# Products of a zero tile in TensorE's waits, k_lo ahead of prod, and VectorE's set-up moved, in a hand-scheduled attention kernel

## What is computed

```python
# stage 0: attention of side (queries) over x (keys, values), plus each query's own key and value
q = (side + b_self) @ Wq + bq
k = concat([x + b_prev, side + b_self]) @ Wk + bk ;  v = concat([x, side]) @ Wv + bv
score_prev = q . k[:256] * SCALE, masked by key position >= seq_len ;  score_self = (q * k[256:]).sum * SCALE
x = x + (softmax([score_prev, score_self]) @ v) @ Wo + bo
# stage 1: pooled mixing of the rows of x
scores = tanh(x @ W1 + b1) @ v ;  mask by the batch's kind (prefix, postfix, all but itself)
x = x + softmax(masked scores) @ x / count
```

## Time and profile before

| quantity | value |
|---|---|
| median of three runs | 279.0 us |
| time of the profiled execution | 281.62 us |
| span of its profile, first to last instruction | 279.9 us |
| TensorE busy with matmuls | 238.4 us, 85% |
| VectorE busy | 184.4 us, 66% |
| ScalarE busy | 156.6 us, 56% |
| GpSimd busy | 76.3 us, 27% |
| mean granted TensorE clock | 0.95 of full speed |

### The profile page before, as it was taken

The page is one execution under the profiler, slowest core; times in us unless marked ns, Lnnn a source line. Parts: engine busy times, 40 slices in busy tenths (PEclk is TensorE's granted clock), DMA queues, the critical chain, the costliest instruction groups (busy, mean ns, idle before and its releaser), DMA issues.

```text
span 279.9 us, 6089 instructions
## 1 busy us (share of the span) xinstructions
PE 238.4 (85%) x2100; PEld 187.4 (67%) x2100; DVE 184.4 (66%) x384; ACT 156.6 (56%) x297; POOL 76.3 (27%) x87
## 2 busy tenths in 40 slices
PE   2986898599979999999999989999999769886732
PEld 2984787367758777877788768777787455563622
DVE  2659655457469758875887588758985885335631
ACT  4351223376477557755785667557856546772430
POOL 8026011013025103610451035103511330316111
PEclk9999669599999999999999999999999997999977
DMA  5469636913865096609560946096409410011011
GB/s 152 103 235 233 138 112 182 210 31 115 242 142 188 5 248 134 228 16 252 119 227 20 256 108 225 18 246 118 150 33 261 95 72 2 8 34 37 0 40 37
DMA packets 28021, 35.50 MB, mean 127 GB/s; under 512 B 4440, under 2 KB 24416, under 8 KB 28000
## 3 DMA queue, kind: packets, MB, share of 16 engines
q1 hardware_dynamic: 27360, 33.12, 44.6%
q0 software_dynamic: 640, 2.10, 2.0%
HBM read 20.26 MB, written 14.69 MB: 125 GB/s over the span
## 4 chain that ended last, share of the span: by engine, by line
PE 59%; DVE 13%; DMA 9%; issue 8%; ACT 5%; SPq 3%; POOL 1%; ACTq 0%; DVEq 0%; POOLq 0%
PE ps_any L1080 20%; PE ps_any L1134 10%; PE ps_max L1108 9%; PE ps_any L1087 6%; DMA k_rows<-k_spill 5%; PE ps_exp L1121 4%; DVE s_max L887 4%; DMA k_spill<-k_lo 3%; PE ps_any L1184 3%; PE ps_any L1240 2%; DVE bv_cast L854 2%; SPq L418 1%; ACT pt L623 1%; PE ps_any L1200 1%; PE ps_any L1166 1%
## 5 line engine op out<-in xcount | busy, mean ns | idle before, releaser
L887 DVE TENSOR_REDUCE s_max<-ps_max 128x4 f32<-128x1024 f32 x64 | 78.1, 1220 | 25.1 <-PE ps_max L1108 25.1
L623 ACT ACTIVATE pt<-ps_exp 128x1024 f32<-128x1024 f32 x64 | 65.6, 1025 | 50.1 <-PE ps_exp L1121 49.5
L1108 PE MATMUL ps_max<-k_rows,q_rows 49*128 49x256 f32 x256 | 33.7, 343 | 13.0 <-DMA k_rows<-k_spill 7.2
L1108 PEld LDWEIGHTS ps_max<-k_rows,q_rows 49*128 49x128 f32 x256 | 20.2, 194 | 24.6 <-DVE s_max L887 10.4
L1134 PE MATMUL ps_any<-pt,v_aug 128*32 128x256 f32 x512 | 36.0, 401 | 0.0
L1121 PE MATMUL ps_exp<-q_rows,k_rows 51*128 51x256 f32 x256 | 27.0, 288 | 2.3 <-ACT pt L623 2.3
L578 POOL TENSOR_TENSOR attn<-num,rden 128x256 f32<-128x256 f32 x16 | 9.6, 621 | 54.0 <-DVE rden L1030 54.0
L1121 PEld LDWEIGHTS ps_exp<-q_rows,k_rows 51*128 51x128 f32 x256 | 20.3, 191 | 4.1 <-ACT pt L623 2.7
L569 POOL TENSOR_TENSOR prod_lo<-prod,prod_hi 128x512 fp32r<-128x512 f32 x8 | 10.3, 1282 | 42.2 <-ACT prod_hi L714 42.2
L1080 PE MATMUL ps_any<-st_hi,w_hi 128*128 128x256 f32 x64 | 20.9, 326 | 0.3 <-DVE st_lo L912 0.3
L1134 PEld LDWEIGHTS ps_any<-pt,v_aug 128*32 128x32 f32 x512 | 13.7, 112 | 10.5 <-issue 1.3
(11 more groups left out here) (145 smaller groups left out, 605.3 us busy)
## 6 DMA issues: line engine op xcount, KB each, us to landing
q_rows<-q_spill SPq DMA_DIRECT2D x32, 192.0 KB, 4.4
k_rows<-k_spill SPq DMA_DIRECT2D x32, 192.0 KB
q_spill<-q_hi SPq DMA_DIRECT2D x16, 256.0 KB, 2.5
k_spill<-k_hi SPq DMA_DIRECT2D x16, 256.0 KB, 2.5
s_sb<-in_fside_BxSxS SPq DMA_DIRECT2D x8, 256.0 KB, 3.7
x_sb<-in_x SPq DMA_DIRECT2D x8, 256.0 KB, 3.2
q_spill<-q_lo SPq DMA_DIRECT2D x8, 256.0 KB, 2.2
k_spill<-k_lo SPq DMA_DIRECT2D x8, 256.0 KB, 3.1
```

The source lines that it names most:

```text
L623: nc.scalar.activation(pt[:, 2 * j % 8:2 * j % 8 + 2], ps_exp[:], ACT.Exp).then_inc(p_ready, 1)
L887: nc.vector.tensor_reduce(s_max[:, j // MJ, :, :, j % MJ].rearrange("p t e -> p e t"), ps_max[:], AX.X, ALU.max).then_inc(max_found, 1)
L1108: last = pe.matmul(ps_max[:, e, t], q_rows[par][rows, j, P * t:P * t + P], k_rows[par][rows, j, :], start=True, stop=True)
```

## The change

1. VectorE zeroes a new tile `idle` (128 x 256) as its first instruction. `idle_products(n)` multiplies it by itself n times on TensorE, into a bank that nobody reads then. The table `IDLE` names where: 13 before the first transposes of the program, 10 after step 1 of period -1, 10 at the end of period -1, 10 after step 4 and 16 after step 13 of period 8, 10 after step 0 of period 9. 16 more stand before the first scores of batch 1, and for this the wait for `max_found` in `scores_for_max` moves ahead of the waits for `q_placed` and `k_placed`.
2. `k_lo` becomes an entry of its own at step 7, ahead of `group_max0` and `prod` at step 8.
3. VectorE's set-up goes from the end of period -1 into period 0: `cast_bv` at step 2, `weight_lo(3)` at step 4, `bias_out` at step 6, `setup_pooling` at step 10. `bv_product` goes to step 5 of period 0 on TensorE.

```diff
-    "st_lo": (1, 1), "xt_lo": (3, 1), "prod": (8, 1), "group_max0": (8, 0), "group_max1": (16, 0),
+    "st_lo": (1, 1), "xt_lo": (3, 1), "k_lo": (7, 1), "prod": (8, 1), "group_max0": (8, 0), "group_max1": (16, 0),
+IDLE = {(-1, -1): 13, (-1, 1): 10, (-1, 15): 10, (8, 4): 10, (8, 13): 16, (9, 0): 10}
+IDLE_BEFORE_SECOND = 16
...
-                    if first and s == STEPS:
-                        cast_bv()
-                        weight_lo(3)
-                        setup_pooling()
-                        dve.wait_ge(bv_product_ready, 1)
-                        nc.vector.tensor_tensor(bias_out[:], bo_wide[:], ps_exp[:, 0, 0], ALU.add
-                                                ).then_inc(bias_out_done, 1)
+                    if isinstance(i, int) and 2 * i + k == 0:
+                        if s == 2:
+                            cast_bv()
+                        if s == 4:
+                            weight_lo(3)
+                        if s == 6:
+                            dve.wait_ge(bv_product_ready, 1)
+                            nc.vector.tensor_tensor(bias_out[:], bo_wide[:], ps_exp[:, 0, 0], ALU.add
+                                                    ).then_inc(bias_out_done, 1)
+                        if s == 10:
+                            setup_pooling()
...
+                    for c in at("k_lo", i, k, s):
+
+                        dve.wait_ge(k_hi_done, count(*c, 1, 1))
+                        if (n := count(*c, 48, 0)) is not None:
+                            dve.wait_ge(k_spilled, n)
+                        for m in range(2):
+                            last = nc.vector.scalar_tensor_tensor(
+                                out=k_lo[:, m], in0=ps_any[:, bank_of("K", *c), m],
+                                scalar=bqk_col[:, 1, m:m + 1], in1=k_hi[:, m].bitcast(F32),
+                                op0=ALU.add, op1=ALU.subtract)
+                        last.then_inc(k_lo_done, 1)
...
+            nc.vector.memset(idle[:].bitcast(F32), 0.0).then_inc(idle_set, 1)
             weight_lo(0)
...
                 par = k % 2
+                if (n := count(i, k, NJ, j)) is not None:
+                    pe.wait_ge(max_found, n)
+                if j == 0 and isinstance(i, int) and 2 * i + k == 1:
+                    idle_products(IDLE_BEFORE_SECOND, ps_max[:, 1, 1])
                 if j % MJ == 0:
                     pe.wait_ge(q_placed[j // MJ], count(i, k, 32, 32))
                     pe.wait_ge(k_placed[j // MJ], count(i, k, 48, 48))
-                if (n := count(i, k, NJ, j)) is not None:
-                    pe.wait_ge(max_found, n)
...
+            def idle_products(n, out_of):
+                for _ in range(n):
+                    pe.matmul(out_of, idle[:, 0:P], idle[:], start=True, stop=True)
+
+            def idle_behind(i, k, s):
+                if isinstance(i, int):
+                    n = IDLE.get((2 * i + k, s), 0)
+                    idle_products(n, ps_exp[:, 1, 1] if i < 0 else ps_max[:, 1, 1])
...
+                    if isinstance(i, int) and (2 * i + k, s) == (0, 5):
+                        bv_product()
...
-                if first:
-                    bv_product()
-
+                    idle_behind(i, k, s)
+
+            pe.wait_ge(idle_set, 1)
+            idle_behind(-1, 1, -1)
             pe.wait_ge(ident_ready, 1)
```

More of the change, by code:

```diff
@@ L170, in build @@
         headsum = sb("headsum", [P, NJ], F32R)
+        idle = sb("idle", [P, S], F32R)
         len_i = sb("len_i", [B, 1], I32)
@@ L269, in build @@
         headsum_ready = sem("headsum_ready")
+        idle_set = sem("idle_set")
         x_loaded = [sem(f"x_loaded{i}") for i in range(2)]
@@ L988, in period @@
                         last.then_inc(prod_done, 1)
[L990 to L998, removed]
                     for c in at("masked", i, k, s):
```

## The result

The changed kernel takes 283.47 us (median of 4, 282.75 to 285.97) beside 278.74 us for the kernel before in the same comparison (median of 4, 276.62 to 279.12): ratio 1.020, 95% interval 1.012 to 1.029. The prediction was 275.3 us. Four executions say little here: 145 executions of the kernel before, taken beside the experiments, run from 277.0 to 287.7 us with a mean of 280.9 and a standard deviation of 2.2, and 12 more of the changed kernel have a mean of 283.3 beside 281.5. All 16 of the changed kernel have a mean of 283.5. So the loss is about 2.6 us, 0.9%; within its own two comparisons, by the means, it is 5.6 us (4 executions each) and 1.8 us (12 beside 35).

What follows compares the result with a forecast made beforehand. TensorE's work made most of the chain, so gains lay at its two ends, where the clock is low: period 0 -0.6, batch 1 -1.8, tail -1.3, sum -3.7 us, from the 279.0 median to 275.3 us; range 271.3 to 278.0.

Steps and rivals of the forecast that it cites:

- setup_pooling at step 10: VectorE, period 0: set-up covered by TensorE's 3.15 us wait for batch 1's rows; otherwise 2.5 us or so once.
- The 16 products: Before batch 1's first scores: 2.1 us of filling fits the 3.15 us wait and the clock holds, -1.8 us.
- is free: Before batch 1's first scores: moving the max_found wait ahead costs nothing, as all three waits had to be met anyway.
- 0 us for six periods: Loop, step 7: k_lo, about 0.8 us, fits VectorE's 1.20 us wait for KS' ahead of prod; no gain.
- The start: Program start: prod 1.6 us earlier through a higher clock, but full DMA queues leave -0.5 us for the first scores.
- the terms of period 0: First scores -0.5, set-up gone from before the maxima -0.6, bv product +1.7, clock's earlier return -1.2: -0.6 us.
- The clock near 30 us: Period 0: clock falls again, more likely than not; an earlier return takes half of 2.3 us, -1.2 us.
- rival A: Period 0: the clock holds there too, -6.5 us in all, 272.5 us; chance 0.28.
- bv_cast: VectorE, moved to period 0 step 2: some tenths of a us, under 1 us, instead of 4.64 us.
- the bv product: TensorE, among period 0's products: +1.1 us at the upper level, about +1.7 at the lower; 1.7 counted.
- The tail: Periods 8 and 9: fillings cost +0.4 us, the held clock gives -1.7 us; together -1.3 us.
- D: Rival: zero products do not raise or hold the clock and only cost, +2.4 us, 281.4 us; chance 0.07.

Runs made afterwards that it cites:

- the last kernel: The kernel before plus 75 products of 16 columns of a zero tile behind TensorE's last work: ratio 1.028, mean 289.3 us.
- the gap: The changed kernel with setup_pooling behind the last maxima of period 0 instead of at step 10: ratio 0.994, mean 280.5 us.
- the 8 wide ones: The change with setup_pooling behind period 0's last maxima, k_lo back behind prod, half as many zero products of 512 columns: ratio 0.995, mean 280.0 us.

## Why the prediction was wrong

**setup_pooling at step 10: the failed step.** The prediction put it down as covered by "the wait of TensorE for batch 1's rows (3.15 us)". It does not stand in that wait but ahead of max5, and that wait begins only behind max7. Its cover at step 10 was VectorE's own slack, and the prediction gave no number for that: before, VectorE waited 0.60 us ahead of max5, 1.72 ahead of max6 and 0.60 ahead of max7, and `setup_pooling` takes 3.6 us in the changed kernel. In the change and its repeat, in the change without the 16 and in the one without zero products, TensorE waits 1.73 to 1.76 us for that `s_max`; with either setup_pooling or k_lo moved back it is 0.19 us or less. With k_lo back TensorE had waited 0.94 us one product group earlier, as in the kernel before, the clock had fallen behind that (42.8 and 43.1 us), and VectorE then kept up with a slower TensorE. Whether the set-up had a part in that fall is not shown: it came at 43.3 to 45.0 us in three traces with the set-up elsewhere too.

The traces put the loss where both parts are. The first half of batch 2's maxima comes to SyncE's queue at 97.2 us in the mean of the four traces with both (96.1 to 98.8), at 94.8 in the two with setup_pooling at step 10 only, at 94.7 in the four with k_lo at step 7 only (93.3 to 95.6), and at 95.1 in the ten with neither (93.2 to 97.6): +2.1 us for both, nothing for one.

The times tell the same of the two together, but also show a loss for each alone, which no trace accounts for. Grouping all executions but those of the last kernel by k_lo at step 7 in all periods and setup_pooling at step 10, whatever else is in them (standard errors worked out from 2.2 us per execution, the comparisons' own levels left aside):

| | executions | mean us |
|---|---|---|
| both | 34 | 283.4 ± 0.4 |
| setup_pooling at step 10 only | 24 | 282.5 ± 0.5 |
| k_lo at step 7 only | 42 | 282.0 ± 0.3 |
| neither | 96 | 281.0 ± 0.2 |
| the kernel before | 145 | 280.9 ± 0.2 |

The setup_pooling step is not the whole miss. The forecast was -3.7 us and the measurement +2.6, 6.3 us apart; with the call in the gap about 3.0 us of that are gone, and the three versions built so with all fillings (36 executions) have a mean of 280.4 beside 280.6. The forecast gain is missing from them too. Parts of it are named below (0.8 us in the transfers, 0.4 outside the span, where it occurs); the rest, about 2 us, stays open.

**The 16 products: the filling works where it is on time at the upper level; the first step made it late.** Forecast -1.8 us. That they take 2.1 us and fit is true in the five traces in which VectorE was on time and the clock stood at the upper level: 2.17 and 2.18 us. Being on time is not enough: the 8 wide ones took 3.70 us, with setup_pooling in the gap, as the clock had fallen at 43.3 us. From mt_sb of batch 0 to that of batch 1, first halves, the six traces that have the 16 (or 8 wide ones) and no set-up at step 10 take 25.9 us in the mean (25.0 to 28.2), the eight with neither 27.4 (25.8 to 28.8): -1.5 us, with a standard error of 0.6. With the set-up at step 10 and the 16, three traces take 28.1. That the wait for max_found "is free" fails with it: it ties the filling to VectorE, so that a late maximum makes the filling late at the lower level, and then it stands in front of rows that are there (55.34 against 52.51 us above). Even so it was no worse than none: without the 16, the same stretch of the change took 29.2 us, with the clock low for 13.7 us of it, against 28.0 with them.

**k_lo: "0 us for six periods" holds for the loop's waits, not for the times.** A fit of all executions with one term each for k_lo, set-up, head and tail products, and the level of each comparison, gives, with 95% intervals, k_lo +1.0 ± 0.7 us and setup_pooling at step 10 +1.4 ± 0.8; the other two are 0 within 0.9. One term each is a rough account: k_lo alone cost 3.3 and 1.7 us against the kernel before, but with setup_pooling in the gap the two versions that differ in k_lo alone have 280.5 and 280.7 us. The place in the loop is as forecast: the waits of TensorE from 96 to 206 us are the same four lines with the same numbers in the kernel before and in the second trace of k_lo alone, which has two of 0.2 us besides. Only period 0 shows a trace of it, `k_lo` in the chain above. Behind group_max0 (step 8) or in period -1 only it costs 0.2 ± 1 us. That it is group_max0's lateness in period 0 fits these, but is argued and not shown.

**The start.** K's products did run at the upper level ahead of 19 us, and the k_lo spill was issued at 19.12 instead of 20.63. The -0.5 us for the first scores did not come in this trace, where they are 0.4 later: the spill took 5.32 us to land and then the rows 3.62. Over ten traces with head products they start at 27.7 us in the mean (26.8 to 28.6), over ten without at 28.1 (26.9 to 29.3): -0.4. That fits the term, but the spread in each group is over four times as wide, so it is not shown by these. As far as the first half of batch 0's maxima the change had won 0.4 us (41.59 against 41.99 us at SyncE's queue), where the terms of period 0 gave 0.6.

**The clock near 30 us.** It fell at 27.8 us in the changed kernel, as forecast (in the ten traces with the 10 products, or 5 wide ones, behind period -1 it fell between 25.6 and 27.9 us, so rival A never came up). It fell inside the wait of 4.77 us that followed the filling, not behind transposes and scores as the prediction had it; so it was in nine of the ten, and in the tenth the fall came 0.1 us into the first scores. The rule of the Trainium skill that I had weighed ("TensorE: Matmul & The Clock Gate", Part 4), that transposes don't count as busy for the clock gate, is therefore not tested by the changed kernel: the transposes come after the fall. bv_cast took 0.48 us, as forecast, and the bv product 1.13 at 35.17, at the upper level, where 1.7 had been counted.

**The tail: right in every trace, not found in the times.** From the transposes of `attn` (258.74) to the issue of the output (276.69) the change takes 17.95 us, before 276.26 - 256.82 = 19.44: -1.5, forecast -1.3. The ten other traces with the tail products have 17.91 to 17.95. Of the nine without them six have 19.42 to 19.44, and three in which the clock fell at other places have 18.97, 18.98 and 20.21. Yet the tail products alone moved the mean by -0.7 us, the version with the gap and the tail only by +0.7, and the fit gives -0.2 ± 0.8 us for them. Why a stretch that is 1.5 us shorter in the traces leaves the time where it was stays open.

**Where the rest of the clock's gain went.** With head products TensorE waits longer for k_rows later, in the loop, where nothing was changed. The waits of TensorE from 96 to 206 us in the version with the gap and k_lo back:

```profile
PE ps_max L1121 <- DMA k_rows<-k_spill: 2.1, 4, 1.1
```

and with the tail products alone:

```profile
PE ps_max L1117 <- DMA k_rows<-k_spill: 0.2, 1, 0.2
```

(us in total, times, longest). Over ten traces with head products this sum is 1.2 us in the mean, over ten without 0.3, and from batch 2's mt_sb to batch 6's they take 112.5 against 111.7 us. So about 0.8 us of what the head won is given back in the loop, in waits for transfers. Why these land later was not settled.

A last part is outside the span. It is 1.61 to 1.74 us in every execution of every kernel of the experiments with up to 6240 instructions, and 2.2 to 3.0 us in 36 of 76 with 6260 (in all four of the change's first). In the mean that is 0.4 us. The version with wide products, with the same filling and 6176 instructions, is free of it, which speaks against the clock as its cause; whether it is the length of the program stays open, since the kernel that was to tell had only 6240.

The prediction named two of these itself as what would make it wrong: "the set-up at step 10 holds up max5 to max7 by more than TensorE's wait", and windows that "are one draw of many". It priced the first at "2.5 us or so once" if the cover were gone, near the loss that came, and put neither the price nor a chance of it into the sum or the range. Its chance of 0.07 for slower was attached to a mechanism that did not occur (D).

## What to carry to other kernels

Work on one engine is covered by a wait of another only if it stands behind the last thing that the other needs from it; look for the row of the engine's own idle time and put it there (here one call moved from step 10 to step 16 gave back 3 us). Filling for the clock that is queued behind a semaphore which the rest of the change can make late loses its gain (3.66 us instead of 2.17, and work behind it that was ready). And where executions scatter by 2.2 us, changes of 1 us need dozens of them and the trace's own waits, not a median of four.

## What the runs showed that I had not expected

The clock's falls are a draw of each execution. The changed kernel's own two traces show it: in the first the clock was low from 27.8 and 48.3 us, in the second from 25.6, 46.1, 80.2 and 227.0. Over the 145 executions of the kernel before, time and mean granted clock go together (correlation -0.69), so the falls account for about half of the variance. In period 7, where the program is the same in nearly all these kernels, the clock was low for 0, 3.4 or 10.2 us. The page's line of zero products alone, and of the version with the gap:

```profile
PEclk9999599999889999999999999999999985899997
```

```profile
PEclk9998699999979999999999999999999999999997
```

The first is low for 10.2 us from 228.3, the second not at all there. From mt_sb of batch 6 to the span's end, traces without tail products took 71.2 to 71.7 us with no fall in period 7 (three), 72.9 to 73.2 with one of 3.4 us (three), 74.2 with another at 260 us besides, and 75.5 with one of 10.2: a spread as wide as any effect looked for. The kernel before and k_lo alone again happened to draw falls at the same moments (50.3 and 50.2 us, 231.2 and 231.1, 268.7 both), and their batch 6 came to SyncE's queue at 207.02 and 207.20 us.

The products of 16 columns start 112 ns apart at the upper level and 213 ns apart at the lower, in a row of 75 that took 12.89 us; products of 256 columns take 0.13 and 0.22 us. Small products are no cheap filling: a sixteenth of the columns saved next to nothing.
